# Three layers on one core: the gate of the feed-forward layers given out over three steps, and what follows it one step later

## What is computed

```python
gating = softmax(x @ W_gate.T)                 # 16 heads
idx = argmax(gating)
indicator = one_hot(idx, H)
gating_top1 = indicator * max(gating)
q, k, v = split(x @ W_qkv.T, 3)                # k, v as 16 heads of 16
k_shared = einsum('bth,bthd->btd', indicator, k)
v_shared = einsum('bth,bthd->btd', gating_top1, v)
att = softmax(where(causal, q_heads @ k_shared.T / sqrt(hd), -inf))
y = att @ v_shared                             # all 16 heads share k and v
```

## Time and profile before

| what | us |
|---|---|
| median of 3 runs | 965.73 |
| lowest and highest of them | 964.95, 966.29 |
| the profiled execution | 963.84 |
| its span, first to last instruction | 962.1 |
| PE busy | 888.4 (92%) |
| DVE busy | 731.0 (76%) |
| ACT busy | 534.9 (56%) |
| POOL busy | 389.2 (40%) |

### The profile page before, as it was taken

The page is one execution under the profiler, slowest core; times in us unless marked ns, Lnnn a source line. Parts: engine busy times, 40 slices in busy tenths (PEclk is TensorE's granted clock), DMA queues, the critical chain, the costliest instruction groups (busy, mean ns, idle before and its releaser), DMA issues.

```text
span 962.1 us, 20249 instructions
## 1 busy us (share of the span) xinstructions
PE 888.4 (92%) x6774; PEld 695.6 (72%) x6774; DVE 731.0 (76%) x2373; ACT 534.9 (56%) x1410; POOL 389.2 (40%) x560
## 2 busy tenths in 40 slices
PE   5789998989999999978999999999999997999996
PEld 4576776767767776657888888787878776777763
DVE  5668988889888998665776768685867677899973
ACT  5636554543345454536667575757575761555555
POOL 4458888886535443352212112020202000444445
PEclk9879999999999999999999999999999999999999
DMA  6333333332112645001202020201102021132321
GB/s 200 60 55 55 55 46 55 54 53 38 35 35 58 133 112 140 2 17 41 45 1 45 1 44 2 45 6 41 28 18 45 2 34 34 37 62 48 73 47 35
DMA packets 51287, 46.63 MB, mean 48 GB/s; under 512 B 6624, under 2 KB 48624, under 8 KB 51184
## 3 DMA queue, kind: packets, MB, share of 16 engines
q1 hardware_dynamic: 51184, 45.34, 23.2%
HBM read 11.40 MB, written 2.10 MB: 14 GB/s over the span
## 4 chain that ended last, share of the span: by engine, by line
PE 36%; DVE 12%; issue 4%; ACT 1%; POOL 0%; DMA 0%; POOLq 0%; SPq 0%; ACTq 0%; DVEq 0%
PE bank L285 9%; PE bank L1904 5%; PE bank L1854 5%; PE bank L1912 4%; PE bank L1842 3%; DVE weights L1418 3%; DVE q_lo L1398 2%; PE bank L1677 2%; PE bank L1689 2%; DVE weights L1408 2%; PE bank L1674 1%; DVE arena L1246 1%; PE bank L1715 1%; ACT oT L943 1%; PE bank L1718 1%
## 5 line engine op out<-in xcount | busy, mean ns | idle before, releaser
L1246 DVE TENSOR_REDUCE arena<-bank 128x2 f32<-128x512 f32 (+1 forms) x192 | 129.1, 680 | 27.0 <-PE bank L1677 26.5
L885 ACT ACTIVATE weights<-bank 128x512 f32<-128x512 f32 x144 | 85.8, 597 | 114.6 <-PE bank L1689 113.7
L964 ACT ACTIVATE weights<-weights,neg_max 128x128 f32<-128x128 f32 (+1 forms) x256 | 113.8, 449 | 19.6 <-DVE neg_max L1408 19.6
L1408 DVE CUSTOM_DVE_ANT_0 weights<-bank,arena 128x128 f32<-128x128 f32 (+1 forms) x256 | 80.7, 353 | 56.5 <-PE bank L1904 54.7
L695 POOL TENSOR_SCALAR_AFFINE_SELECT weights<-weights 128x256 f32<-128x256 f32 x144 | 68.1, 474 | 126.4 <-ACT weights L885 126.2
L971 ACT ACTIVATE weights<-bank 128x384 f32<-128x384 f32 x128 | 62.9, 491 | 85.4 <-PE bank L1912 83.2
L1677 PE MATMUL bank<-kf_stack,q_stack 96*128 96x128 f32 (+1 forms) x512 | 109.6, 317 | 0.0
L1904 PE MATMUL bank<-kbT,arena 128*128 128x128 f32 (+1 forms) x512 | 105.1, 328 | 1.1 <-DVE y L420 0.9
L648 POOL TENSOR_SCALAR weights<-weights 128x512 f32<-128x512 f32 x64 | 97.9, 1539 | 13.3 <-ACT weights L788 13.0
L1418 DVE TENSOR_SCALAR weights<-weights,inv_sum 128x128 f32<-128x128 f32 (+1 forms) x256 | 83.8, 369 | 4.5
L285 PE MATMUL bank<-x_hi,wb_hi 128*128 128x256 f32 x256 | 83.6, 326 | 2.8 <-DVE q_lo L1398 2.8
(11 more groups left out here) (228 smaller groups left out, 2379.4 us busy)
## 6 DMA issues: line engine op xcount, KB each, us to landing
q_stack<-q_hi SPq DMA_DIRECT2D x96, 128.0 KB, 3.8
arena<-arena SPq DMA_DIRECT2D x64, 128.0 KB, 2.5
q_stack<-q_lo SPq DMA_DIRECT2D x48, 128.0 KB, 4.0
ka_stack<-k_hi SPq DMA_DIRECT2D x32, 76.5 KB, 3.5
x_all<-x SPq DMA_DIRECT2D x8, 256.0 KB, 5.1
st_wo<-b_wo SPq DMA_DIRECT2D x8, 256.0 KB, 3.7
arena<-b_wqn SPq DMA_DIRECT2D x8, 256.0 KB, 3.2
out<-x_all SPq DMA_DIRECT2D x8, 256.0 KB, 2.1
```

Of the source, the lines that this page charges most:

```text
L964: last = a.activation(p, p, ACT.Exp, scale=-1.0, bias=neg_max[:, h % 4, t:t + 1], accum_out=sums[:, h % 4, t:t + 1])
L1246: v.tensor_reduce(into, p1[k % 2][:, :].rearrange("p (h k) -> p h k", h=n), AX.X, ALU.max, negate=True).then_inc(s["maxed"], 1)
L1408: last = v.tensor_tensor_reduce(out=probs[:, h % 4, part], in0=ps_s[h % 2][:, part], in1=mask_b[:, (1 - t) * P:2 * P], scale=1.0, scalar=F ...
```

## The change

```diff
@@ GpSimd, ffn step
-                    if k == 8 and there(b + 1):
+                    if k == 10 and there(b + 1):
                         keys_of_f(b + 1)
@@ VectorE, prepare_f
                         gate(5, v.tensor_tensor(g_eq, lg, top, ALU.is_equal))
+                    elif k == 7:
                         gate(6, v.tensor_tensor(g_eq, g_eq, cst[:, C_DESC:C_DESC + H].unsqueeze(1)
                                                 .to_broadcast([P, NT, H]), ALU.mult))
                         gate(7, v.tensor_reduce(g_s[:, :, 1], g_eq, AX.X, ALU.max))
+                    elif k == 8:
                         gate(8, v.tensor_tensor(g_hot, g_eq, g_s[:, :, 1:2].to_broadcast([P, NT, H]), ALU.is_equal))
                         pick(0, ps_a[:, 0:D], g_hot).then_inc(s["k_sel"], 1)
-                    elif k == 7:
                         pick(1, ps_b[:, 0:D], g_hot).then_inc(s["k_sel"], 1)
-                    elif k == 8:
+                    elif k == 9:
                         dve.wait_ge(*at(s, "k_sel", b, 2))
...
                                         ALU.add).then_inc(s["k_sel"], 1)
+                    elif k == 10:
                         dve.wait_ge(*at(s, "gate_exp", b, 1))
...
-                    elif k == 9:
                         dve.wait_ge(*at(s, "gate", b, 11))
...
-                    elif k == 10:
+                    elif k == 11:
                         dve.wait_ge(*at(s, "v_sel", b, 1))
@@ TensorE, prepare_f and step
-                    elif k == 8:
+                    elif k == 9:
                         pe.wait_ge(*at(s, "k_sel", b, 1))
...
-                    elif k == 10:
+                    elif k == 11:
                         pe.wait_ge(*at(s, "k48", b, 3))
...
-                    if k == 10 and there(b + 2):
+                    if k == 11 and there(b + 2):
...
                         pe_transpose_x(s, b + 2)
```

## The result

| | kernel before | changed kernel |
|---|---|---|
| median of 5 runs (lowest to highest), us | 966.29 (964.95 to 970.81) | 973.12 (970.57 to 973.92) |
| profiled execution: time, span, us | 963.84, 962.1 | 970.78, 969.1 |
| ratio | 1 | 1.0053 (95%: 1.0032 to 1.0073) |

The ratio is formed from the runs and is not that of the two medians, which stand 6.8 us (0.7%) apart. In a second session the ratio was 1.0039 (1.0022 to 1.0055), with medians of 966.56 and 970.50. So by the ratios the change costs 4 to 5 us, between 0.4 and 0.5%. The forecast of 966.5 was too low, and so was its range up to 970.3: the first median lies 2.8 us above it, that of the second session 0.2.

What follows compares the result with a forecast made beforehand. TensorE was taken to bound the 19.20 us period, apart from VectorE's gate block. Nine transitions +3.6, into batch 7 -0.6, edges -1.2, -0.6, -0.4 and 0 gave +0.8 us: forecast 966.5 us, range 963.2 to 970.3.

Steps and rivals of the forecast that it cites:

- Part 4: Both groups of transposes at the end of step 11: TensorE stalls 0.91 us a period for kf_stack, a loss.
- Part 1: VectorE's gate in pieces, steps 6 to 8: line 1700 starts earlier, a gain of 0.6 us a period.
- Part 2: V projection after step 9's attention product instead of before step 9's scores: cost taken as 0, up to 0.3 a period.
- Into batch 7: Last transition of each ffn layer, with no next x to transpose: 0.3 us gained, twice, -0.6 in all.
- Edge (a): First ffn layer, into batch 2: scores of step 11, attention a's guards and x_lo come earlier, -1.2 us.
- Rival A: Slower: the ScalarE stall comes at every transition and the edges give nothing; +4 to +5 us, 970.2, chance 0.26.
- Edge (b): Second ffn layer, batch 0: VectorE, the bound up to x_lo, loses its 0.49 wait for the V projection, -0.6 us.
- Edge (c): Last head of attention b: the V projection falls beside TensorE's 0.85 idle for oT, an estimated -0.4 us.
- Edge (d): First layer into batches 0 and 1, inside attention a: gains and losses cancel, 0, bounds -0.8 and +1 us.
- Parts 2 and 3: V projection a step later, and GpSimd's small key operations two steps later, covered by nearly 2 us: each costed at 0.
- Rival C: The new 0.9 us stop lowers TensorE's clock in each period: some +1.2 us each, 977; chance 0.04 with other new waits.

## Why the forecast was wrong, step by step

**Part 4 held.** It was given 0.91 for the stall and 0.1 for the other order. Measured: 0.93 in all, from step 10 to step 0. The chain from the start of x's transposes to the mask takes 1.61 (325.32 to 326.93), forecast 1.56. The wait that the trace names is 0.73, since TensorE's own transposes fill 0.88 of it by the profile and not the 0.65 that I subtracted. It stands in ten transitions.

**Part 1 is the mis-sized term of the period.** It was -0.6 and measured -0.37. By the trace line 1701 did come 0.62 us earlier (12.97 against 13.59 from step 0). But the text called the maximum of step 7 "just covered", and said that 0.2 more would take 0.2 of the gain. It ended 0.18 us after line 1701 began, and the mask behind it started 0.24 after line 1701, where before the next product came after 0.02. The V projection, which Part 2 moved from between the two, had been the cover; Part 2 was costed at 0 and is where the loss comes from. So the step that failed is the cover of the maximum of step 7: put at 0, measured 0.24 us a period. The right sum for a period is -0.62 + 0.24 + 0.93 = +0.55, not +0.4. Over eight transitions the miss is 1.15 us. Into batch 7, where the same mask stands behind line 1701, the change gave 0.15 instead of 0.3.

**Edge (a)** gave 0.5 of its 1.2. It counted on the wait of 0.66 at step 8 going. That wait moved one mask on, to step 9:

```profile
279.01 0.39 PE L1675 MATMUL bank<-mask_bf,ident_bf 128*128 128x512 bf16 x1 [0.65 <-DVE arena L1246]
```

So x_lo (line 341) starts 24.15 us behind the mask of batch 1's step 0 (287.92) where it was 24.66: 0.51 earlier, not over a microsecond. The wait of the projection of q for x_lo (1.07 us at 286.49 before) is gone, and one row of TensorE ahead of it stands the kf_stack stall in full:

```profile
287.28 0.39 PE L1675 MATMUL bank<-mask_bf,ident_bf 128*128 128x512 bf16 x1 [0.73 <-ACT kf_stack L914]
```

With the transition behind it the edge was forecast at -0.8 and measured at +0.04. Rival A had this: "TensorE reaches x_lo's reader with kf_stack late".

**Edge (b)** gave 0.38 of 0.6. The wait of 2.29 is now 1.26:

```profile
813.86 0.28 PE L1675 MATMUL bank<-mask_bf,ident_bf 128*128 128x256 bf16 x1 [1.26 <-DVE arena L1246]
```

Against the second trace of the kernel before it gave nothing: into batch 1 that trace took 16.85 us, the changed ones 16.92 and 16.91.

**Edge (c)** gave more, 0.9 for 0.4: the V projection now stands where the 0.85 at 795.02 was, and the shift against the kernel before falls from 5.7 us (789.58 against 795.31, line 1854/1855) to 4.8 (795.99 against 800.80, line 1912/1913). A smaller wait came for it in the head before:

```profile
797.35 0.87 PE L1843 MATMUL bank<-weights,kv_tok 128*64 128x256 f32 x8 [0.58 <-ACT weights L971]
```

The longer clock fall at 412 hides the gain: the shift rises by 1.34 us from line 1700 there (412.00 against 416.06) to the wait for q_lo (423.55 against 428.95), and the added matmuls gave 1.3. **Edge (d)** was put at 0 with a bound of +1, and measured +0.9, in both traces of the changed kernel (0.91 and 0.92). Most of it is line 407's wait for oT, 0.58 and 0.69 us before (236.57 and 260.60), 0.75 and 1.21 in the changed kernel (238.52 and 263.28).

**Parts 2 and 3** cost nothing by themselves at their own places: the V projection and GpSimd's keys (line 683 at 323.04, 2.8 us ahead of the keys' transposes) make nobody wait.

**What no step had.** +1.8 us of the profiled span arose ahead of the change and belongs to that execution; the forecast was made against one span and could not know it. The clock behind the 412 us wait was in no step. Rival C had the clock in the wrong place: ten stops of 0.73 us left it at 1.00 through the steady stretches, for example

```profile
320.00:330.00 10.00, 9.27 (x79) 6.52 (x77) 9.28 (x21) 4.69 (x10) 4.46 (x10) 1.00 0.72 159
```

The six transposes directly ahead of each stop did not bring it down either. By the rule of the Trainium skill cited with rival C ("TensorE: Matmul & The Clock Gate", "Part 4: PE-mode transpose") they would have added to the stop; these traces show nothing of it.

**The sum.** Of the 6.2 us between +0.8 and +7.0, 1.8 are the start of that execution, 1.3 the clock behind 412, 1.3 the periods (with the one behind edge (a)), 0.9 edge (d), 0.7 edge (a) and 0.5 edge (b) and batch 7; edge (c) gives 0.5 back (0.2 is rounding and a rest between the layers).

Rival A's number came out: +4 to +5 by its own sum, +3.8 to +5.1 by the ratios. Its mechanism did so in part. The stall at every transition, what it said of edge (a), and (d) were right. But it was to decide if the three edges returned under 1 of 2.2 us, and they returned 1.8 against the first trace (0.5, 0.4 and 0.9). What filled the gap, 0.57 a period and the clock at 412, it did not have, so its number is in part luck. The forecast fell short because each move was priced by the wait that would go, and none by the wait that would come next.

**What stays open.** Why the clock behind the same wait of 2.3 us at 412 us lost 3.4 us in eight traces (both of the changed kernel, the gate over two steps, the gate with the later sum, the keys inside step 11 with the later sum, and the three with both groups inside step 11, keys first), 1.7 in seven (both of the kernel before, the transposes alone, both groups inside step 11 with x first, the gate over three steps, the keys inside step 11, the same with sum and tie-break moved) and nothing in one (keys first at the end of step 11). Neighbouring kernels fall into different groups, so it need not be a matter of the code. Further, why the clock fell at 288 in two runs, and when the weights are late.

## What to carry to other kernels

When work moves out from between two instructions of an in-order engine, ask what it covered: the second instruction's wait appears there in full, here 0.24 us a period behind a term costed at 0. Ask it of small waits too: one that ends together with the instruction ahead is named in no view, and only the releaser's end shows it. A wait that goes at an edge is a gain only after the next instruction's own wait has been priced in the new order. And where a stall is a chain over two engines, try the exchange of neighbours first: the keys ahead of x, on both engines, was worth 6 to 7 us here by the ratios (1.0039 to 0.997) and needed nothing else.

## What the runs showed of the hardware

- After the same wait of 2.3 us TensorE's granted clock fell to its lower level (1.2 of 2.4 GHz) for a time that lost 3.4 us in eight traces, 1.7 in seven and nothing in one. It fell once more behind a wait of 1.26 us at 813.86 (0.64 at 816 to 820 in the changed kernel). Ten stops of 0.73 us, one every 19.8 us with matmuls in a row between them, never lowered it.
- With six matmuls of constants in the wait of 2.3 us the clock stayed at 1.00 there (416 to 424 in the changed kernel). In all four such traces it fell at the next long wait, of 2.06 us, and lost 1.7 us; of the six traces of these kernels without them one has a fall there.
- Two executions of the same instructions differ by up to 1.34 us in the first 196 us (197.61 against 196.27), and by 2.4 us between the layers (418.15 against 420.53), where one waited 1.1 us for weights and had a second fall of the clock. That is as much as most of the terms of this prediction.
- Turning the keys (two transposes) between two score products took 0.14 us from start to start (323.30 to 323.44). Where the next instruction waited for VectorE's pick it took 0.42 (362.32 to 362.74), and the view named no wait.
